# Two experts' scatters interleaved by halves, gathers issued earlier, and nine staging buffers in a fused convolution and expert-choice layer

## The reference

```python
t = _to_tokens(x)                       # 16 * 784 tokens of 128
logits = x_flat @ Wr                    # x_flat = layer norm of t
probs = jax.nn.softmax(logits, axis=0)  # over all tokens
vals, idx = jax.lax.top_k(probs.T, C)   # each of 8 experts takes C = 1024 tokens
selected = x_flat[idx]
h = gelu(einsum('ecd,edf->ecf', selected, W1) + b1)     # 128 -> 512
out_e = einsum('ecf,efd->ecd', h, W2) + b2              # 512 -> 128
weighted = vals[..., None] * out_e
output = zeros_like(x_flat).at[idx.reshape(-1)].add(weighted.reshape(-1, Dd))
t = t + output
```

## Time and profile before

| | |
|---|---|
| median of 3 runs | 476.32 us (475.66 to 480.82) |
| profiled execution | 479.45 us; span of its instructions 477.4 us |
| PE busy | 349.9 us (73%) |
| DVE busy | 315.1 us (66%) |
| ACT busy | 256.3 us (54%) |
| POOL busy | 159.5 us (33%) |
| hardware DMA queue of SP | 63.77 MB, 42.3% of 16 engines |
| software DMA queue of POOL | 8.72 MB, 12.2% of 16 engines |
| DMA, mean over the span | 160 GB/s |

### The profile page before, as it was taken

How to read it: one execution, slowest core, us unless ns; L and a number is a source line. 1 busy time by engine, 2 the same in 40 slices (tenths; PEclk the granted TensorE clock), 3 DMA queues, 4 the chain that set the end, 5 groups by cost and what they waited for, 6 DMA issues and landing times.

```text
span 477.4 us, 7763 instructions
## 1 busy us (share of the span) xinstructions
PE 349.9 (73%) x2459; PEld 242.4 (51%) x2459; DVE 315.1 (66%) x1047; ACT 256.3 (54%) x526; POOL 159.5 (33%) x151
## 2 busy tenths in 40 slices
PE   2878999999999978311225869797989199778663
PEld 2435656566656657200112545573756187466552
DVE  3378897799999886788787585657563122473544
ACT  3359898789999873676601554363645143612000
POOL 4000000000000000000037777787888778865300
PEclk9989998999999995555555997998989589989955
DMA  4446577577666643892012232444535997338998
GB/s 109 122 124 182 186 232 247 172 249 226 219 230 222 213 151 132 270 382 91 0 23 55 53 98 53 94 37 98 75 49 77 271 309 139 42 27 201 241 369 313
DMA packets 39121, 76.19 MB, mean 160 GB/s; under 512 B 7056, under 2 KB 19504, under 8 KB 39088
## 3 DMA queue, kind: packets, MB, share of 16 engines
q1 hardware_dynamic: 28128, 63.77, 42.3%
q0 software_dynamic: 9472, 8.72, 12.2%
q10 hardware_dynamic: 1488, 3.30, 1.9%
HBM read 35.03 MB, written 30.39 MB: 137 GB/s over the span
## 4 chain that ended last, share of the span: by engine, by line
PE 43%; DVE 19%; ACT 17%; issue 9%; DMA 7%; SPq 3%; POOL 2%; DVEq 0%; ACTq 0%; POOLq 0%
PE psC L894 11%; PE psC L731 7%; ACT ln_tok L541 4%; PE psB L882 4%; PE psC L882 4%; PE psB L761 3%; DMA out_dram<-hid 3%; DVE work L1040 2%; ACT x_in L601 2%; PE psB L749 2%; PE psD L791 2%; ACT signs L601 2%; PE psA L894 2%; DMA x_in<-token_rows,slot_idx 1%; DMA hid<-x_pad 1%
## 5 line engine op out<-in xcount | busy, mean ns | idle before, releaser
L438 POOL DMA_INDIRECT picked<-token_rows,slot_idx x32 | 31.9, 996 | 248.3 <-issue 247.9
L731 PE MATMUL psC<-x_pad,tap_diag 64*64 64x392 f32 x384 | 72.2, 524 | 7.7 <-issue 3.9
L731 PE MATMUL psC<-hid,tap_turned 64*64 64x392 f32 x384 | 72.2, 525 | 0.0
L894 PE MATMUL psC<-w,hid 128*128 128x128 f32 x448 | 53.8, 283 | 1.8 <-ACT hid L659 1.7
L894 PEld LDWEIGHTS psC<-w,hid 128*128 128x128 f32 x448 | 52.9, 199 | 4.3 <-ACT hid L659 3.4
L731 PEld LDWEIGHTS psC<-x_pad,tap_diag 64*64 64x64 f32 x384 | 29.6, 141 | 38.8 <-issue 31.9
L1362 DVE TENSOR_TENSOR y_sum<-psC,b_rows 128x512 f32<-128x512 f32 x14 | 9.7, 691 | 48.0 <-PE psC L894 48.0
L541 ACT ACTIVATE ln_tok<-psA,sm 112x128 f32<-112x128 f32 x112 | 40.8, 477 | 0.9 <-DVE sm L1032 0.9
L659 ACT ACTIVATE hid<-psB,b_T 128x512 f32<-128x512 f32 x32 | 21.7, 685 | 35.5 <-PE psB L882 35.5
L464 POOL DMA_INDIRECT moe_sum<-y_rows,slot_idx x24 | 37.6, 1567 | 7.3 <-issue 6.7
L882 PE MATMUL psB<-picked_T,w 128*128 128x512 f32 x64 | 35.9, 689 | 5.0 <-ACT picked_T L629 3.1
(11 more groups left out here) (254 smaller groups left out, 798.5 us busy)
## 6 DMA issues: line engine op xcount, KB each, us to landing
token_rows<-rows SPq DMA_DIRECT2D x16, 422.6 KB, 4.8
x_in<-in_x_dram SPq DMA_DIRECT2D x16, 392.0 KB, 3.3
x_res<-in_x_dram SPq DMA_DIRECT2D x16, 392.0 KB, 4.0
moe_sum<-hid SPq DMA_DIRECT2D x16, 392.0 KB, 4.5
x_all<-work SPq DMA_DIRECT2D x16, 392.0 KB, 2.9
moe_sum_late<-hid SPq DMA_DIRECT2D x16, 392.0 KB, 6.4
w<-in_L_ffn_W_dram SPq DMA_DIRECT2D x16, 256.0 KB, 3.3
hid<-x_pad SPq DMA_DIRECT2D x32, 120.0 KB, 2.5
```

Of the source, the lines that this page charges most:

```text
L438: nc.gpsimd.indirect_dma_start(out=picked_in[k][:, b, :], out_offset=None, in_=rows_dram, in_offset=bass.IndirectOffsetOnAxis(ap=slot_idx[ ...
L731: ins = nc.tensor.matmul(psC[col * HC:col * HC + HC, half, 0:HALF].rearrange("c (h w) -> c h w", w=W), weights[of, n, :], lines[of, q, dy: ...
L894: ins = nc.tensor.matmul((psA if first else psC)[:, h, b * C:(b + 1) * C], hid[:, f, lo:lo + 128], w2[:, q, f * C:(f + 1) * C], start=(f = ...
```

## The change

`LATE_ORDER` numbers 16 blocks of the last two experts in the order 6 first half, 7 first half, 6 second half, 7 second half. `scatter_late` issues a half, after the four blocks before it have landed. `need` counts blocks in that order: a block j of expert 6 is number j for j < 4 and j + 4 from there, one of expert 7 is j + 4 or j + 8. Expert 7's weighted rows go to `y_last` (a picked buffer that is free by then), not to `y_rows`. Gathers of experts 6 and 7 stand earlier in POOL's order, the weights of expert 7 are loaded after eight of the sixteen `load_first`, and PE turns expert 7's first half ahead of expert 6's `down`. The folds of `moe_sum` are in two groups, and there are nine `o_img` buffers. SP issues the loads of images 0 to 7, then six stores, then the rest.

```diff
@@ L52
...
 SECOND = E // 2
-FOLD_SPOTS = (range(0, 4), range(4, 10), range(10, B))
+FOLD_SPOTS = (range(0, 10), range(10, B))
 STORED_BY_SP = 8
+LATE_ORDER = [(e, b) for half in range(2) for e in (E - 2, E - 1) for b in range(4 * half, 4 * half + 4)]
 LAST_TILES = (TPI - 1) * B
...
@@ L222
...
             s_cmp[0:P, :, :].rearrange("p b k -> p (b k)")]
-        o_img = [hid[:, k:k + 1, 0:HW] for k in range(ENDS)]
+        y_last = picked[:, 1, :, 0:C]
+        hid_flat = hid[:, :, :].rearrange("c f n -> c (f n)")
+        o_img = [hid_flat[:, k * HW:(k + 1) * HW] for k in range(5)] + [
+            w1[:, :, :].rearrange("c q n -> c (q n)")[:, 0:HW], w2[:, :, :].rearrange("c q n -> c (q n)")[:, 0:HW],
+            picked_T[:, 0:HW], y_sum[:, :, :].rearrange("c b n -> c (b n)")[:, 0:HW]]
+        STAGED = len(o_img)
         end_regions = (psB, psD, psA, psC)
...
@@ L369
...
             for img in range(B):
+                if img == B // 2:
+                    sp.wait_ge(s_l2, (E - 2) * 2)
+                    load_w(E - 1, (E - 1) % 2)
                 load_first(img)
-            sp.wait_ge(s_l2, (E - 2) * 2)
-            load_w(E - 1, (E - 1) % 2)
-
-            sp.wait_ge(s_sca[0], 16 * SB * E // 2)
-            sp.wait_ge(s_sca[1], 16 * SB * (E // 2 - 1))
-            sp.wait_ge(s_need, 2)
+
+            for q in range(2):
+                sp.wait_ge(s_sca[q], 16 * SB * (E // 2 - 1))
+            sp.wait_ge(s_need, 7)
...
                 at = LAST_TILES + img
-                sp.wait_ge(s_landed, sp.value_load(need[at:at + 1, 0:1], min_val=1, max_val=SB))
+                sp.wait_ge(s_landed, sp.value_load(need[at:at + 1, 0:1], min_val=1, max_val=2 * SB))
                 sp.dma_start(sums_in[img].rearrange("p (t c) -> p t c", c=C),
-                             late_t[:, ds(img, 1), :, :].rearrange("p i t c -> p (i t) c")).then_inc(s_yl[img], 16)
-
-            for img in range(B):
+                             late_t[:, ds(img, 1), :, :].rearrange("p i t c -> p (i t) c")).then_inc(s_yin[img], 16)
+
+            def store(img):
+                sp.wait_ge(s_fa, img + 1)
+                sp.dma_start(out_d[:, img, :], o_img[img % STAGED]).then_inc(s_fo[img % STAGED], 16)
+
+            for img in range(B // 2):
                 load_late(img)
-                if img >= B - STORED_BY_SP:
-                    stored = img - (B - STORED_BY_SP)
-                    sp.wait_ge(s_fa, stored + 1)
-                    sp.dma_start(out_d[:, ds(stored, 1), :], o_img[stored % ENDS]).then_inc(s_fo[stored % ENDS], 16)
-            sp.wait_ge(s_landed, SB)
-            for k in range(ENDS):
-                sp.wait_ge(s_fo[k], 16 * B // ENDS)
+            for img in range(STORED_BY_SP - 2):
+                store(img)
+            for img in range(B // 2, B):
+                load_late(img)
+                if img < B // 2 + 2:
+                    store(STORED_BY_SP - 2 + img - B // 2)
+            sp.wait_ge(s_landed, 2 * SB)
+            for k in range(STAGED):
+                sp.wait_ge(s_fo[k], 16 * len(range(k, B, STAGED)))
             for q in range(2):
...
@@ L427
...
-            def gather(e, half):
+            def gather(e, half, some=range(4)):
                 k = e % BUFS
...
                 pool.sem_inc(s_pool, 1)
-                for b in range(4 * half, 4 * half + 4):
+                for b in some:
+                    b += 4 * half
                     nc.gpsimd.indirect_dma_start(
...
@@ L454
...
+
+            def scatter_late(e, half):
+
+                pool.wait_ge(s_yr, e * 2 + half + 1)
+                if (e, half) == (E - 2, 0):
+                    pool.wait_ge(s_sca[1], 16 * SB * (E // 2 - 1))
+                first = LATE_ORDER.index((e, 4 * half))
+                for k in range(max(first - 4, 0), first):
+                    pool.wait_ge(s_blk[k], 16)
+                pool.sem_inc(s_pool, 1)
+                for b in range(4 * half, 4 * half + 4):
+                    nc.gpsimd.indirect_dma_start(out=late_dram,
+                                                 out_offset=bass.IndirectOffsetOnAxis(ap=slot_idx[:, e, b:b + 1], axis=0),
+                                                 in_=y_rows[:, 0, b, :] if e == E - 2 else y_last[:, b, :], in_offset=None,
+                                                 compute_op=ALU.add).then_inc(s_blk[LATE_ORDER.index((e, b))], 16)
...
@@ L479
...
             gather(6, 0)
+            gather(6, 1)
             scatter(3)
-            gather(6, 1)
+            gather(7, 0)
             scatter(4)
-            gather(7, 0)
+            gather(7, 1, range(0, 2))
             scatter(5)
-            gather(7, 1)
-            scatter(6)
-            scatter(7)
+            gather(7, 1, range(2, 4))
+            scatter_late(6, 0)
+            scatter_late(7, 0)
+            scatter_late(6, 1)
+            scatter_late(7, 1)
...
@@ L924
...
                         turn_picked(e + 1, h)
+                else:
+                    turn_picked(e + 1, 0)
                 pe.wait_ge(s_w2[q], use * 16 + 16)
...
 ...
@@ L941
...
                 pe.wait_ge(s_w1[q], use * 16 + 16)
+                hidden(e, q, 0, {})
+                pe.wait_ge(s_w2[q], use * 16 + 16)
+                down(e, q, 0)
                 pe.wait_ge(s_idx, E * 2)
...
                     turn_first(img)
-                turn_picked(e, 0)
+                turn_picked(e, 1)
                 pe.wait_ge(s_fk, 2 * FOLD_SPOTS[0].stop)
-                hidden(e, q, 0, {})
-                pe.wait_ge(s_w2[q], use * 16 + 16)
-                down(e, q, 0)
-                for img in FOLD_SPOTS[1]:
-                    turn_first(img)
-                turn_picked(e, 1)
-                pe.wait_ge(s_fk, 2 * FOLD_SPOTS[1].stop)
                 hidden(e, q, 1, {})
                 down(e, q, 1)
-                for img in FOLD_SPOTS[2]:
+                for img in FOLD_SPOTS[1]:
                     turn_first(img)
...
@@ L1306
...
+                number, turn = (1, 3) if e == E - 2 else (2, 4)
+                done = 0 if e == E - 2 else 3
...
-                nc.vector.tensor_scalar(need[last, :], s_edge[last, 1:2], 1.0, 127.0, ALU.max, ALU.add).then_inc(s_need, 1)
-                dve.wait_ge(s_need, 1)
-                nc.vector.tensor_scalar(need[last, :], need[last, :], 7, None, ALU.logical_shift_right).then_inc(s_need, 1)
+                nc.vector.tensor_scalar(need[last, 0:1], s_edge[last, 1:2], 1.0, -1.0, ALU.max, ALU.add).then_inc(s_need, 1)
+                dve.wait_ge(s_need, done + 1)
+                nc.vector.tensor_scalar(need[last, turn:turn + 1], need[last, 0:1], 7, 4, ALU.logical_shift_right, ALU.bitwise_and)
+                nc.vector.tensor_scalar(need[last, number:number + 1], need[last, 0:1], 7, None, ALU.logical_shift_right)\
+                    .then_inc(s_need, 1)
+                dve.wait_ge(s_need, done + 2)
+                if e == E - 2:
+                    nc.vector.scalar_tensor_tensor(need[last, 1:2], need[last, 1:2], 1.0, need[last, 3:4], ALU.add, ALU.add)\
+                        .then_inc(s_need, 1)
+                else:
+                    nc.vector.scalar_tensor_tensor(need[last, 2:3], need[last, 2:3], 5.0, need[last, 4:5], ALU.add, ALU.add)\
+                        .then_inc(s_need, 1)
+                    dve.wait_ge(s_need, done + 3)
+                    nc.vector.tensor_tensor(need[last, 0:1], need[last, 1:2], need[last, 2:3], ALU.max).then_inc(s_need, 1)
...
@@ L1365
...
-                if since(e, 2):
+                if since(e, 2) and e < E - 1:
...
-                nc.vector.tensor_tensor(y_rows[:, q, 4 * h:4 * h + 4, :], y_sum[:, 4 * h:4 * h + 4, :],
+                to = y_last if e == E - 1 else y_rows[:, q, :, :]
+                nc.vector.tensor_tensor(to[:, 4 * h:4 * h + 4, :], y_sum[:, 4 * h:4 * h + 4, :],
...
@@ L1414
...
-                for img in FOLD_SPOTS[0]:
-                    add_first(img)
...
+                    if h == 1:
+                        norm_picked(e, 1)
...
@@ L1424
...
                     weigh(e, q, use, h)
-                    if h == 0:
-                        norm_picked(e, 1)
-                    for img in FOLD_SPOTS[1 + h]:
+                    for img in FOLD_SPOTS[h]:
                         add_first(img)
...
             dve.wait_ge(s_fk, 2 * B)
-            dve.wait_ge(s_l2, 2 * E)
+            dve.wait_ge(s_yr, 2 * E)
...
             for img in range(B):
-                k = img % ENDS
+                k = img % STAGED
                 dve.wait_ge(s_ft, img + 1)
-                if img >= ENDS:
-                    dve.wait_ge(s_fo[k], img // ENDS * 16)
+                if img >= STAGED:
+                    dve.wait_ge(s_fo[k], img // STAGED * 16)
                 for a, (lo, n) in enumerate(((0, 4 * P), (4 * P, 3 * P))):
-                    ins = nc.vector.tensor_tensor(o_img[k][:, 0, lo:lo + n], end_regions[k][:, a, 0:n],
```

(28 more changed lines are left out.)

## The result

The changed kernel is about 1% slower: 481.84 us median (477.75 to 487.28, 20 runs) against 478.17 us (472.21 to 480.82, 20 runs) for the kernel before; ratio 1.0097, 95% interval 1.0069 to 1.0124. The forecast was 475.8 us, 470 to 481.

The account below looks back on a forecast made before the run. The end was taken as bound by the late scatters' landings, then by full DMA engines moving image loads and stores. Terms -0.3 and -0.2 gave -0.5 us, put on the 476.32 median: 475.8 us, range 470 to 481.

Parts of the forecast that it names:

- k = 12: First late scatter block of expert 7's second half on POOL; forecast issue at 442.7, 3.3 us later than before.
- 25 transfers: Loads of images 7 to 15 and all 16 stores, left at image 7's load; 27.1 us at 371 GB/s.
- Waits 2, 3 and 5: POOL's waits for landings before scatter 6 first half (0 us), 7 first half (2.3) and 7 second half (2.3).
- Wait 4: POOL before scatter 6 second half: previous blocks land beside loads of images 0 to 6; 4.4 us, bounds 2.3 and 5.1.
- The 8.0 us: Alternative sum of POOL's waits, with 2.0 us for each of three exposed late hand-overs, in place of 11.0.
- Wait 1: POOL before expert 5's scatter: expert 4's scatter must have landed; 2.0 us, kept 0 to 3.4.
- Work: POOL's blocks up to k = 12, the same as before: 78.4 us, nothing saved.
- -0.3: SP's load of image 7 goes at 446.2 against 446.54, as k = 12 lands in quiet: -0.3 us.
- The last stretch: From image 7's load to the end: 30.86 us before, changed by the term Together -0.2.
- Together -0.2: After image 7's load: -0.9 us from buffers and SP's burst of stores, +0.7 from three scatter blocks instead of two.
- The slower rival: Landings beside loads or stores take 5.4 to 7 us at hand-overs 1, 4, 5 and k = 12; 481.2 us, chance 0.15.
- The faster rivals: POOL's hand-overs land in quiet: 470.8 us, chance 0.24; or staging (DVE's waits for stores) was the limit: 466, chance 0.03.

Follow-up runs that it names:

- a1: The changed kernel with SP's six stores of images 0 to 5 ahead of image 7's load; ratio 1.0034 to the kernel before.
- e1: The changed kernel with `moe_sum` loads of images 8 to 15 held until expert 4's scatter landed, and six stores ahead of image 7's load; ratio 1.0046.
- c1: The changed kernel with experts 6 and 7 scattered whole and SP's loads and stores in pairs from image 8 on; ratio 1.0061 to the kernel before.
- c2: c1 with `moe_sum` loads of images 8 to 15 held until expert 4's scatter has landed; ratio 1.0037 to the kernel before.
- f3: c2 with four staging buffers instead of nine; ratio 1.0019 to the kernel before.
- j1: c1 with four staging buffers and all sixteen `moe_sum` loads held until expert 4's scatter has landed; ratio 1.0025 to the kernel before.
- h1: c2 with all sixteen late loads issued ahead of SP's eight stores; ratio 1.0040 to the kernel before.
- a2: The changed kernel with SP's order of the kernel before: a load, then one store, in pairs from image 8 on; ratio 1.0094.
- g1: The kernel before with nine staging buffers and nothing else; ratio 1.0032 to the kernel before.
- a3: The changed kernel with no late load on SP before the first eight late scatter blocks have landed; ratio 1.0134 to the kernel before.
- i1: The changed kernel with all sixteen `moe_sum` loads held until expert 4's scatter landed, expert 7's weights ahead of them; ratio 1.0112 to the kernel before.
- d1: The changed kernel with `moe_sum` loads of images 8 to 15 held until expert 4's scatter has landed; ratio 1.0045 to the kernel before.

## Why the prediction was wrong

**What held.** PE's 10.4 us and both waits for y_rows went; image 7 waits for k = 12; SP keeps six stores behind it; 25 transfers are left then. Waits 2, 3 and 5 were 0, 2.4 and 2.3 us as forecast.

**Wait 4: 4.4 forecast, 5.3 measured.** The landing was right (6.3 us). The step that failed is "so the next block could come 6.3 - 1.86 = 4.4 us late": from the landing to the next block's start POOL needs 0.88 us more. 6.28 + 0.88 - 1.86 = 5.3. It could have been seen before. The block ahead of 427.66 is this one (timeline of POOL before):

```profile
423.49 1.55 POOL L464 DMA_INDIRECT moe_sum_late<-y_rows,slot_idx  x1 [0.30 <-issue]
```

From start to start that is 4.17 us, while a block in quiet lands after 3.3 to 3.4. Waits 3 and 5 were taken from this measured wait, 0.8 to 0.9 us included, and came out right; 1 and 4 were worked out from landings. The 8.0 us that the prediction sets beside its sum has the same kind of slip the other way: it takes a whole landing for a wait, without the 1.86 us of the step.

**Wait 1: 2.0 forecast, 3.7 measured.** The same 0.88 was left out, and of two neighbours I took the middle. Scatter 4's last block, issued at 386.76, landed after some 6.7 us (394.30 - 0.88 - 386.76, an estimate), nearly the 7.14 of the row in full traffic. Both measured waits lie outside the bounds that I had kept.

**Work: 78.4 forecast, 79.0 measured.** Together k = 12 is 6.6 us later than the old fifth block, not 3.3. Its landing (3.3 us for 7) gave back 3.8, as forecast: image 7's load is 2.8 us later, where -0.3 stood in the sum.

**The last stretch: 30.7 forecast, 33.3 measured.** The term "Together -0.2" failed as a whole, and was +2.4. Set against 1.08 us for each transfer left (25; 19 in a1 and e1; 27 in c1, c2, f3 and j1, where images 5 and 6 are loaded just ahead and 10.9 MB move instead of 10.1 to 10.3), the stretch is longer by 3.1 to 4.2 us in seven traces with whole scatters, and by 4.9 to 6.7 in all eight with halves. (h1's, set aside above, has whole scatters and 5.6, with all its loads ahead of the stores.) Without that count: a2 has the transfers and SP's order of before and g1, and takes 32.3 us against 30.9 and 30.7. So it goes with the halves, and not visibly with buffers or the order of stores. With halves, blocks 14 and 15 are issued only after image 7's load (448.51 and 450.37) and land after 6.7 and 6.8 us; I had priced one more block at 0.7 us of engines. That these blocks are the cause fits, but no run isolates them, so the cause of this part stays open.

The price itself, 371 GB/s for full engines, was no constant either. In the changed kernel the share is 1.01 at 464 to 467 with 239 GB/s, when the loads of images 11 to 15 have been issued one after another; in a2, with loads and stores in pairs, it is 1.03 with 408 GB/s at the same distance from image 7's load. But a2's last 4.9 us have 152 GB/s, and it gains nothing by it.

**The sum.** +2.8 and +2.4 make +5.2 us, where -0.5 was forecast. Of the 5.7 us between them the waits 1 and 4 are 2.6, the work 0.6 and the last stretch 2.6. The slower rival, "scatter blocks beside loads or stores take 5.4 to 7 us", named the mechanism and its places 1 and 4; it got 0.15 because I asked for it at all four places at once. That its 481.2 us lie so near the measured time is luck: at its places 5 and k = 12 nothing stretched (2.3 and 3.3 us), and the last stretch made up for that. The faster rivals have no support: no landing was quiet where traffic ran, and staging was not the limit.

## What to carry to other kernels

A scatter split into alternating pieces that must not overlap pays one landing per hand-over, and the landing is longest exactly when the loads it was meant to release run beside it. Holding these loads back moved the wait to the next hand-over (a3, i1). What helped on POOL was fewer hand-overs (8.0 us in c1), though it only won back the loss; work between a piece and the one that waits for it hides a landing, as the two gather blocks between scatters 5 and 6 did. Price a hand-over from issue to next issue, not from issue to landing, and look in the data for the one item that crosses the half, before a queue is put behind it.

## What the hardware showed

A scatter block of 128 rows lands 3.3 us after its issue in quiet, and after 6.3 to 6.8 us where loads or stores of 392 KB run beside it all the time; the eight blocks of scatter 5 in i1, beside the sixteen loads, took 9.2 to 10.1 us. From landing to the next indirect DMA on POOL another 0.88 us pass. DMA engines at a share of 1.0 moved between 239 and 410 GB/s, by what was in flight. The start of POOL's gather 6 varied from 343.7 to 351.2 us between executions whose program ahead of it is the same (d1 and a3), more than the change is worth, so traces had to be compared from a common event.
